# The second layer's q, k and v projections: matrix products of 16 bit halves, rows turned by DMA, and the rotation in whole banks

## The reference, cut to what matters

```python
x_even = x[..., 0::2]
x_odd = x[..., 1::2]
y_even = cos * x_even - sin * x_odd
y_odd = sin * x_even + cos * x_odd
...
B, S, D = (2, 512, 256)          # 16 heads of 16 features; here 4096 rows
k = jnp.arange(d_k // 2, dtype=jnp.float32)
inv_freq = theta ** (-2.0 * k / d_k)
```

## Time and profile before

| | us |
|---|---|
| median of 3 runs | 4289.29 (4286.6 to 4293.62) |
| the profiled execution's own time | 4291.54 |
| span of its trace | 4289.8 |
| the stage of the change, first issue to the next stage's first matmul | 2156.53 to 2269.19 |
| TensorE clock granted over the span | 0.947 |

### The profile page before, as it was taken

One profiled execution on the slowest core, in us unless ns is written; L12 is line 12 of the kernel. 1 busy time (PEld: TensorE's weight loads), 2 busy tenths in 40 slices (PEclk: granted clock), 3 DMA queues, 4 the chain that ended last, 5 costly groups with the idle time before them and its releaser, 6 DMA issues. The chain is left out here.

```text
span 4289.8 us, 95023 instructions
## 1 busy us (share of the span) xinstructions
PE 3826.2 (89%) x38376; PEld 2155.0 (50%) x38376; DVE 3321.8 (77%) x5451; ACT 2577.8 (60%) x3482; POOL 1197.4 (28%) x966
## 2 busy tenths in 40 slices
PE   7999999679988869998986999999999999866996
PEld 4888888535555535555553332332333333334664
DVE  5788888779985469985687899999998978584444
ACT  5566666546554336553443677787888887644553
POOL 2123231277761067761140000000000000033552
PEclk8999999889999989999997999999999999977998
DMA  4011110133320033330072000000000000034664
GB/s 102 13 32 34 37 34 16 46 72 64 61 47 28 0 70 61 64 54 8 0 168 39 9 9 2 9 2 1 9 2 2 9 2 9 5 100 92 119 131 112
DMA packets 343285, 179.58 MB, mean 42 GB/s; under 512 B 256916, under 2 KB 333928, under 8 KB 342376
## 3 DMA queue, kind: packets, MB, share of 16 engines
q1 hardware_dynamic: 320264, 138.08, 15.0%
q0 software_dynamic: 13440, 21.24, 2.8%
q10 hardware_dynamic: 9184, 14.68, 1.3%
HBM read 77.81 MB, written 38.58 MB: 27 GB/s over the span
## 5 line engine op out<-in xcount | busy, mean ns | idle before, releaser
L2327 DVE TENSOR_REDUCE s_tops<-ps 128x2 f32<-128x1024 f32 (+3 forms) x1152 | 1251.8, 1132 | 143.7 <-PE ps L2213 101.5
L2296 ACT ACTIVATE s_weights<-ps 128x1024 f32<-128x1024 f32 (+3 forms) x1152 | 1093.9, 953 | 346.1 <-PE ps L2226 195.3
L2248 PE MATMUL ps<-s_weights,v_flat 128*32 128x256 f32 (+1 forms) x8704 | 695.0, 391 | 6.8 <-ACT s_o_t L2302 5.7
L2226 PE MATMUL ps<-s_q,keys 50*128 50x512 f16 (+3 forms) x2304 | 435.9, 375 | 47.4 <-DVE s_tops L2327 33.1
L2207 PE MATMUL ps<-keys,s_q 48*128 48x512 f16 (+3 forms) x2304 | 436.7, 377 | 42.0 <-DVE s_tops L2327 23.3
L2363 POOL CAST s_shift<-s_minus_top 128x16 f16<-128x16 f32 x32 | 6.3, 196 | 1430.4 <-DVE s_minus_top L2334 1430.4
L653 PE MATMUL ps<-a_qt,a_kt 128*128 128x256 f16 x3072 | 375.3, 273 | 3.9 <-POOL s_ones L608 3.9
L2226 PEld LDWEIGHTS ps<-s_q,keys 50*128 50x128 f16 x2304 | 112.1, 93 | 514.6 <-issue 249.0
L1244 PE MATMUL ps<-attention_w,la_yt 128*128 128x512 f16 x1152 | 292.3, 402 | 37.9 <-DMA la_yt<-la_y_parts 30.5
L653 PEld LDWEIGHTS ps<-a_qt,a_kt 128*128 128x128 f16 x3072 | 300.9, 98 | 40.3 <-POOL s_ones L608 4.1
L1319 ACT ACTIVATE la_weights<-ps 128x1024 f32<-128x1024 f32 x124 | 127.0, 1024 | 302.1 <-PE ps L1234 302.1
(11 more groups left out here) (381 smaller groups left out, 7146.1 us busy)
## 6 DMA issues: line engine op xcount, KB each, us to landing
ex_whole<-in_L_ffn_w_dram ACTq DMA_DIRECT2D x14, 1024.0 KB, 9.9
qk_parts<-a_parts SPq DMA_DIRECT2D x64, 128.0 KB, 4.1
keys<-qk_parts SPq DMA_DIRECT2D x48, 128.0 KB, 5.2
s_q<-qk_parts SPq DMA_DIRECT2D x48, 128.0 KB, 4.6
x<-in_x_dram SPq DMA_DIRECT2D x8, 512.0 KB, 9.0
attention_w<-attention_split SPq DMA_DIRECT2D x2, 2048.0 KB, 9.0
la_table<-in_rotary_dram SPq DMA_DIRECT2D x64, 64.0 KB, 2.1
a_table<-in_rope_dram POOLq DMA_DIRECT2D x8, 512.0 KB, 6.3
```

The lines of the kernel that those rows point to most:

```text
L2226: mm = pe.matmul(m.ps[:, bank, skip:CHUNK], m.keys[rows(half, depth), pair, kt * P:(kt + 1) * P], b.q[rows(half, depth), place % 2, pair, ...
L2248: mm = pe.matmul(m.ps[h * QUAD:(h + 1) * QUAD, OUT, begin:end], m.v_flat[:, first:first + QUAD], weights[:, a % 2, h, begin:end], start=(k ...
L2296: act.activation(weights[:, a % 2, 2 * pair:2 * pair + 2, skip:CHUNK], m.ps[:, bank:end + 1, skip:CHUNK], ACT.Exp).then_inc(s["exp"], 1)
L2327: dve.tensor_reduce(tops[:, u % 2, :, i % 2, t, c], m.ps[:, bank:end + 1, 0:width], AX.X, ALU.max).then_inc(s["max"], 1)
```

## The change

- Normalised rows are divided by 8 and split into two 16 bit halves: the upper one by ACT, the lower one by POOL (`row_low`), for chunk 0 in four pieces and by DVE (`piece_low`). `normed` and `rows16` have one buffer each.
- SP turns them by four DMA transposes a chunk (`turn`); the turns on PE, and ACT's reading back, go.
- The scale is folded into the matrices, which are split too; q's factor 1/4 goes into them. The shift becomes a product of its own (`shifts`), is split (`bias_parts`, `bias_low`), and is added to each output by a seventh matmul.
- Products are six 16 bit matmuls plus that seventh one, where two 32 bit ones were.
- The features are laid out with the first halves of all heads in one bank and the second halves in the next. So DVE makes one instruction over two banks for `straight` and one for `crossed`, and POOL adds or subtracts across the banks (`combine`). Upper and lower halves and the stores also go over two banks. `crossed` has one buffer.

```diff
-        w = sb("w", [P, 3, KD, D])
-        normed = sb("normed", [P, 2, TPC, D])
+        normed = sb("normed", [P, TPC, D])
+        rows16 = sb("rows16", [P, TPC, 2, D], F16)
-        crossed = sb("crossed", [P, 2, CHUNK])
+        crossed = sb("crossed", [P, KD, CHUNK])
...
# SP
+                def turn(c):
+                    if c:
+                        need(sp, s["ht"], 16 * TPC * c)
+                    if c >= 2:
+                        need(sp, s["v_mm"], 2 * (c - 1))
+                    for j in range(TPC):
+                        if c < PIECED:
+                            sp.wait_ge(s["piece_low"], TPC * c + j + 1)
+                        else:
+                            sp.wait_ge(s["row_low"], c - PIECED + 1)
+                        sp.dma_start_transpose(ht[:, c % 2, :, :, j * P:(j + 1) * P].rearrange("p a k t -> p (a k) t"),
+                                               rows16[:, j, :, :].rearrange("p a d -> p (a d)")).then_inc(s["ht"], 16)
+                turn(0)
                 sp.dma_start(m.modb[:, 2:6, :], m.next_modb).then_inc(s["modb_in"], 16)
...
+                turn(1)
...
                 for c in range(CHUNKS):
-                    store(c, c % 2)
+                    if c + 2 < CHUNKS:
+                        turn(c + 2)
+                    store(c)
...
# POOL
+                def row_low(c):
+                    pool.wait_ge(s["row_high"], c - PIECED + 1)
+                    pool.tensor_tensor(rows16[:, :, 1, :], normed[:, :, :], rows16[:, :, 0, :], ALU.subtract).then_inc(s["row_low"], 1)
+                def combine(c):
+                    for g in range(2):
+                        need(pool, s["rot"], 2 * c + g + 1)
+                        first, second = g * KD, g * KD + 1
+                        pool.tensor_tensor(straight[:, first, :], straight[:, first, :], crossed[:, 1, :], ALU.subtract)
+                        pool.tensor_tensor(straight[:, second, :], straight[:, second, :], crossed[:, 0, :], ALU.add).then_inc(s["sum"], 1)
+                load(0, 0)
+                load(1, 1)
+                row_low(1)
                 pool.memset(m.v_flat[:, TILES * V_ROW:], 0.0)
                 pool.memset(m.v17[:, :, :, L1_DH:L1_DH + 1], 1.0).then_inc(s["ones"], 1)
-                ahead_in_pairs(pool, CHUNKS, load, add)
+                for c in range(CHUNKS):
+                    if c + 2 < CHUNKS:
+                        row_low(c + 2)
+                    combine(c)
+                    if c + 2 < CHUNKS:
+                        load(c + 2, c % 2)
...
# DVE
+                def rotate(c, g):
+                    u = c % 2
+                    dve.wait_ge(table_in[u], 16 * (c // 2 + 1))
+                    need(dve, s["mm"], 2 * c + g + 1)
+                    need(dve, s["low"], 2 * (c - 1) + g + 1)
+                    need(dve, s["sum"], 2 * c + g)
+                    pair = slice(g * KD, (g + 1) * KD)
+                    for to, part in ((straight[:, pair, :], 0), (crossed[:, :, :], 1)):
+                        r = dve.tensor_tensor(to, m.ps[:, 2 + g * KD:2 + (g + 1) * KD, :],
+                                              table[:, u, part:part + 1, :].broadcast_to([P, KD, CHUNK]), ALU.mult)
+                    r.then_inc(s["rot"], 1)
+                def low(c, g):
+                    dve.wait_ge(s["high"], 2 * c + g + 1 + CREDIT)
+                    pair = slice(g * KD, (g + 1) * KD)
+                    dve.tensor_tensor(parts[:, pair, 1, :], straight[:, pair, :], parts[:, pair, 0, :], ALU.subtract).then_inc(s["low"], 1)
+                for i in range(3):
+                    fold(i)
+                    piece_low(i)
+                piece_low(TPC - 1)
+                for i in range(3):
+                    weight_low(i)
+                bias_low()
+                for c in range(CHUNKS):
+                    rotate(c, 0)
+                    if c:
+                        low(c - 1, 1)
+                    rotate(c, 1)
+                    low(c, 0)
+                low(CHUNKS - 1, 1)
...
# ACT
+                def whole(c):
+                    need(act, s["ht"], 16 * TPC * c)
+                    for j in range(TPC):
+                        n = normalise(c, j)
                     n.then_inc(s["normed"], 1)
+                    act.wait_ge(s["normed"], c - PIECED + 1)
+                    act.copy(rows16[:, :, 0, :], normed[:, :, :]).then_inc(s["row_high"], 1)
...
+                pieces()
+                for i in range(3):
+                    weight_high(i)
+                bias_parts()
+                whole(1)
                 act.wait_ge(s["ones"], 1)
-                scaled(0, 0)
...
+                for c in range(CHUNKS):
+                    if c + 2 < CHUNKS:
+                        whole(c + 2)
+                    high(c, 0)
+                    high(c, 1)
+                    values(c)
...
# PE
+                def shifts():
+                    pe.wait_ge(s["w_in"], 16 * 3)
+                    pe.wait_ge(s["shift_rep"], 1)
+                    for i in range(3):
+                        for k in range(KD):
+                            mm = pe.matmul(m.ps[:, i // 2, (i % 2) * D:(i % 2 + 1) * D], shift_rep[:, k, :], w[i][:, k, :], start=(k == 0), stop=(k == KD - 1))
+                    mm.then_inc(s["shift_mm"], 1)
                 def products(c, u):
-                        for k in range(KD):
-                            mm = pe.matmul(m.ps[:, 2 + n, :], w[:, n // KD, k, o * P:(o + 1) * P], ht[:, u, k, :],
-                                           start=(k == 0), stop=(k == KD - 1))
-                        mm.then_inc(s["mm"], 1)
+                        for i, (k, p, q) in enumerate(terms):
+                            mm = pe.matmul(m.ps[:, 2 + n, :], w16[:, n // KD, p, k, o * P:(o + 1) * P], ht[:, u, q, k, :], start=(i == 0), stop=False)
+                        mm = pe.matmul(m.ps[:, 2 + n, :], bias16[:, n // KD, o * P:(o + 1) * P], even[:, :], start=False, stop=True)
+                        if o == KD - 1:
+                            mm.then_inc(s["mm"], 1)
...
-    halves = np.arange(D).reshape(D // P, P // L1_DH, L1_DH // 2, 2).transpose(0, 3, 2, 1).reshape(D)
+    halves = np.arange(D).reshape(L1_HEADS, L1_DH // 2, 2).transpose(2, 1, 0).reshape(D)
```

More of the change, by code:

```diff
@@ L1849, in attention1_projections @@
+        shift_rep = m.modb[:, 0, :].rearrange("p (k t) -> p k t", k=KD)
+        size, minus = m.modb[:, 1, 0:TILES], m.modb[:, 1, TILES:2 * TILES]
         ones16 = b.q[0:SHIFT_ROWS, 0, 0, :]
-        with stage(nc, "a1", "w_in", "modb_in", "table_even", "table_odd", "ones", "ones16", "q_in", "minus", "normed", "turned", "ht", "mm", "v_mm", "rot", "sum", "high", "low", "v", "out_0", "out_1", "out_2", "out_3", "ones_in", "keys_in") as (block, s):
-            table_in, parts_out = (s["table_even"], s["table_odd"]), [s[f"out_{n}"] for n in range(OUTS)]
+        with stage(nc, "a1", "w_in", "modb_in", "table_even", "table_odd", "ones", "ones16", "even", "q_in", "size", "minus", "shift_rep", "folded", "w_high", "w_low", "shift_mm", "bias_high", "bias_low",
+                   "piece", "piece_high", "piece_low", "normed", "row_high", "row_low", "ht", "mm", "v_mm", "rot", "sum", "high", "low", "v", "out_0", "out_1", "ones_in", "keys_in") as (block, s):
+            table_in, parts_out = (s["table_even"], s["table_odd"]), [s[f"out_{n}"] for n in range(2)]
@@ new lines, in high, with values @@
+                def high(c, g):
+                    need(act, s["sum"], 2 * c + g + 1)
+                    need(act, parts_out[g], 16 * STORES * c)
+                    pair = slice(g * KD, (g + 1) * KD)
+                    act.copy(parts[:, pair, 0, :], straight[:, pair, :]).then_inc(s["high"], 1)
+                def values(c):
+                    for n in range(2):
+                        need(act, s["v_mm"], 2 * c + n + 1)
+                        act.copy(m.v17[:, bass.ts(c * 2 + n, 2), :, 0:L1_DH],
+                                 m.ps[:, 6 + n, :].rearrange("p (j h d) -> p j h d", j=2, d=L1_DH)).then_inc(s["v"], 1)
@@ L1984, in _ @@
             def _(pe):
-                credit(pe, s["turned"], s["mm"], s["v_mm"])
-                def turn(c, u):
-                    need(pe, s["normed"], c + 1)
-                    for k in range(KD):
-                        need(pe, s["ht"], KD * (c - 1) + k + 1)
-                        for j in range(TPC):
-                            t = pe.transpose(m.ps[:, k, j * P:(j + 1) * P], normed[:, u, j, k * P:(k + 1) * P], m.ident[:, :])
-                        t.then_inc(s["turned"], 1)
+                credit(pe, s["mm"], s["v_mm"])
@@ L2011, in products @@
                         mm.then_inc(s["v_mm"], 1)
-                ahead_in_pairs(pe, CHUNKS, turn, products)
+                shifts()
+                pe.wait_ge(s["w_low"], 3)
+                pe.wait_ge(s["bias_high"], 4)
+                pe.wait_ge(s["bias_low"], 3)
+                pe.wait_ge(s["even"], 1)
```

(1 more changed line is left out.)

155 lines of the change are left out of this document (72 added, 83 removed).

## The result

The changed kernel takes 4332.7 us in the median (4329.4 to 4337.1, four runs) against 4287.9 us (4283.9 to 4293.6) for the kernel before: a ratio of 1.0108, with a 95% interval of 1.0095 to 1.0121. The prediction was 4325, range 4306 to 4345. It is slower, as forecast, and 8 us more than forecast.

The account below looks back on a forecast made before the run. DVE was taken to bound the stage before, and a ring of ACT, POOL and DVE after. Terms 17.4 + 16.8 + 0.2 + 1.8 = 36.2, say 36 us on the median of 4289.3, gave 4325; range 4306 to 4345.

Parts of the forecast that it names:

- What bounds the stage: Before the change DVE bounds the steady chunk, busy 11.83 of 12.2 us, with PE close behind at 11.36.
- the ring: Steady chunks after the change: ACT, POOL and DVE wait for each other in series, 16.0 us a chunk against 12.3.
- The wait for DVE: In each full ring, a POOL add meeting DVE's remainder loses 1.1 us, bounds 0 and 1.24.
- The seven steps, 102.9 and 0.2: First add to first add: five of 16.0, then 10.9 and 12.0, 102.9 us against 86.1; query issues cost 0.2 once.
- the first rival: Transposes wait in the DMA queue behind the keys, costing from 6.1 us on; 18 more, 4343 us; chance 0.12.
- Ahead of the first add, 17.4: From last matrix, shifts, normalisations and transposes in series, POOL's first add comes at 2186.6, 17.4 us late.
- The tail, 1.8: From the last chunk's first add to the next stage: 15.7 us against 13.9, 1.8 more.
- The upper bound: Top of the main case, 4330 us: matrix at 6.0, first transposes landing at 4.0, the full 1.24; 5 more.
- The signs that I named: In the trace: first add near 2186, steps some 16 us apart, POOL's remainder ahead of each, adds 1.25 and one 2.3.
- One sign of being wrong: Prediction counts as wrong if, among others, ACT or POOL idles for DMA in the stage.
- The fall of the clock: PE's pauses lower its clock and PE bounds if below 0.59 in the mean; about 60 more, 4350 us; chance 0.06.
- The ring falling apart: ACT runs ahead, so a chunk takes 9.8 us and the kernel is 7.7 less, 4282 us; chance 0.06.

Follow-up runs that it names:

- run 8: Kernel before with rotation, adds, casts, remainders and stores over two banks, and ACT's normalisation of chunk c+2 ahead of both casts; 4287.2 us, ratio 0.9998.
- Run 3: Changed kernel with a second buffer for the crossed products, whose own load moves to the stage's end; 4312.9 us, ratio 1.0051.
- run 5: Changed kernel with DVE's remainder of each pair replaced by a copy of the pair's high half; 4323.7 us, ratio 1.0087.
- run 1: Changed kernel with POOL's adds of chunk c put ahead of the row remainder of chunk c+2; 4320.9 us, ratio 1.0074.
- run 10: Changed kernel with ten more products of 512 columns a chunk in PE's pauses, into an unread bank; 4338.7 us, ratio 1.0116.
- Run 6: Changed kernel with the ones loaded after chunk 2's transposes and query loads in threes behind the keys of two consecutive chunks; 4325.3 us, ratio 1.0090.
- run 2: Changed kernel with chunk 1's transposes issued ahead of the ones and all twelve query loads moved to the last chunk; 4338.1 us, ratio 1.0111.
- run 4: Kernel before with only the table, rotation, adds, casts, remainders and stores in pairs of banks; 4300.1 us, ratio 1.0023.
- run 9: Changed kernel's half products and wide rotation, but rows turned by PE as before, unfolded weights, two crossed buffers, ACT normalising ahead of its casts; 4287.3 us, ratio 0.9999.
- run 12: Half products, wide rotation, rows turned by PE, with POOL's next halves between the adds, DVE's remainder before rotation, later ones and first tables; 4291.3 us, ratio 1.0010.
- run 7: Changed kernel with two crossed buffers, POOL's row remainder between the two pairs' adds, later ones and queries in threes; 4324.2 us, ratio 1.0089.

## Why the prediction was right, and where its numbers were off

**What bounds the stage.** Right. PE was indeed close behind DVE: run 8 takes 4.8 us a chunk off DVE and gains nothing. And what decides after the change is the order of the queues. Run 3 takes one link out of the ring and the steps fall by 2.5; run 5 shortens one by 0.8 and the steps fall by 0.8; run 1 turns the order of two calls and moves the first add by 13.3; run 10 shows that the clock has no part.

**The ring, 16.0 a chunk.** Measured 15.7. The links are as priced, but for the v copies and the wait: high 0.95, values 0.95 (priced at 1.07), whole 3.15, row_low 2.1, adds 2.5, rotation 2.4, adds 3.4, and 0.25 between them. The wait for DVE was 0.91 instead of 1.1 (2.17 less 1.26), and run 5 gives 0.8 for it by itself. The rule of the Trainium skill that I weighed (page "SBUF — State Buffer", section "SBUF: two separate sides") would have this as a wait for a whole instruction of the other engine, and the trace agrees: the add was held for most of the 1.22 of the remainder.

**The seven steps, 102.9 and 0.2.** Measured 106.5. The plain steps are 1.5 us under the term in all. The 0.2 for the six query issues was mis-sized: that step is 20.8, 5.1 over the others. I had counted 3.75 us of issue time against 3.6 us of spare time, with a landing of 2.5 behind it. But behind twelve loads the last transpose of chunk 5, issued at 2243.24, took 3.0 to issue and landed 7.0 after its start. The landing was the term at fault: 4.5 more, when the queries had used up the spare time. This is the first rival, in one step of seven and with the queries in its queue. Behind six loads of keys alone the transposes landed after 2.5 to 5.0, below the 6.1 from which the rival would have begun to cost. Run 6 takes the step back to 16.3.

**Ahead of the first add, 17.4.** Measured 23.5, the largest error of the sum. `turn(1)`, from its first issue to ACT's next normalisation, took 10.8 instead of 6.6: I had taken the first layer's value, and here the loads of ones stood ahead and made the first two transposes 4.3 longer to issue; the last landed after 2.5 as priced. Runs 2 and 6 give 4.6 and 4.2 for it. The last matrix was there 5.9 us after its issue instead of 4.0, and the wait for chunk 0's transposes ahead of `whole(1)` cost about 0.5 that I hadn't priced. Shifts took 5.4 instead of 6.1.

**The tail, 1.8.** Measured 1.0.

**Sum.** 6.1 too little ahead of the first add, 3.4 too little in the steps, 0.8 too much in the tail: 8.7 us, and the medians differ by 44.8 instead of 36. The upper bound that I gave the case, 4330, was passed by 3 us: it let the first transposes land at 4.0 and had nothing late behind the queries. The stated range holds the result only because it reached out to the first rival.

**The signs that I named.** Steps of 15.7 (four of the five), POOL's remainder ahead of the first add of each, the adds of 1.25 and the one of 2.2 came as written. One sign of being wrong came too: ACT idled for DMA, 18.6 us in three places, 13.1 ahead of the first add and 5.0 in the long step. In the other steps it did not. And that the first add starts at 2187.7, near the 2186 that I wrote, is luck: counted from the stage's start it is 6.0 late, and the stage itself began 4.9 earlier in this execution.

**The rivals.** The fall of the clock: the clock was 0.67 to 0.89 in the steps of the whole ring, above the 0.59 from which it would decide, although PE pauses in every one. The page "TensorE: Matmul & The Clock Gate" of the Trainium skill says in "HAM oscillation — how this bites in real kernels" that such pauses drop the clock again and again; the trace agrees in part (0.67 to 0.89 in the steps; with the pauses filled 1.00 in three of five, 0.78 and 0.89 in the others), and run 10 shows that it cost nothing. The ring falling apart: PE, DVE and ACT did not run ahead; written order held.

## What to carry to other kernels

Before handing an engine new work for a later chunk, write down each engine's order over one period and follow it once round: if the new work waits for something that is queued behind this chunk's last result, its whole duration joins the period, however idle all engines are. That happened in four designs here (the changed kernel with its variants, runs 4, 9 and 12); in runs 4 and 8 the place of one call made all the difference. And when the ring is gone, look at the engine that only issues: in run 7 SP's queue was full at 15.9 us a chunk, just where the ring had been.

## What the runs showed of the hardware that I had not expected

- Two loads into two partitions each (128 KB each, 0.7 us to issue) hold up what is issued behind them on the same queue, until 13 us (changed kernel) or 17 us (run 7) after the first of them was issued: the two transposes behind them took 6.9 us to issue instead of 2.5, with a DMA share of 1.16 at 23 GB/s, and in run 7 four stores behind them took 8.9 us instead of the 2.2 to 3.0 of later chunks and two transposes behind these 6.2.
- A DMA transpose takes SP 1.26 us to issue in the median, but four took 5.7 to 7.2 right behind nine to twelve loads of keys and queries, with most of the excess in the last (1.8 to 3.0), and one took 4.08 behind the ones. So the engine that issues is held up too, with all that stands behind on its queue.
- A one input 16 bit copy on DVE (0.42 us) held an add on POOL by 0.12 at most, the two input remainder (1.22) by 0.91.
